# Forty unread products on TensorE in steps 5 to 9 of the first stage of a Hyena + FFN block

## What is computed

```
xn  = layernorm(x)                               # over the 256 channels
h   = layernorm(xn) * gamma + beta
v, x1, x2 = split(h @ W_in + b_in, 3)            # each 4096 x 256
y   = causal_conv(v, k0) * x1                    # 128 taps per channel, along the tokens
y   = causal_conv(y, k1) * x2
att = xn + y @ W_out + b_out
ffn = (silu(xn @ wg.T) * (xn @ wu.T)) @ wd.T     # hidden 768, int weights times 1/127
out = x + att + ffn
```

## Time and profile before

| what | value |
|---|---|
| median of 3 runs | 351.94 us (351.06 to 352.59) |
| profiled execution | 351.36 us |
| its span | 349.5 us |
| mean granted clock of its span | 0.974 |
| PE busy | 307.8 us (88%) |
| PEld busy | 239.7 us (69%) |
| DVE busy | 247.0 us (71%) |
| POOL busy | 215.7 us (62%) |
| ACT busy | 181.8 us (52%) |

### The profile page before, as it was taken

One profiled execution on the slowest core, in us unless ns is written; L12 is line 12 of the kernel. 1 busy time (PEld: TensorE's weight loads), 2 busy tenths in 40 slices (PEclk: granted clock), 3 DMA queues, 4 the chain that ended last, 5 costly groups with the idle time before them and its releaser, 6 DMA issues.

```text
span 349.5 us, 11796 instructions
## 1 busy us (share of the span) xinstructions
PE 307.8 (88%) x4941; PEld 239.7 (69%) x4941; DVE 247.0 (71%) x498; ACT 181.8 (52%) x379; POOL 215.7 (62%) x302
## 2 busy tenths in 40 slices
PE   0767777776897999999999999999999999998995
PEld 0355666655775777777777777777777876657994
DVE  3996983555357577568567678867766966897895
ACT  3634886954335354443444444434544344549992
POOL 3979999302887888866876776777886782210000
PEclk9965998999999999999999999999999999999999
DMA  7990260006687957879578687786786969400445
GB/s 236 349 357 21 70 235 4 0 9 232 241 311 255 388 194 308 314 250 387 206 304 345 249 366 247 288 356 229 333 304 262 381 240 344 169 0 2 164 140 180
DMA packets 21506, 81.01 MB, mean 232 GB/s; under 512 B 1479, under 2 KB 12619, under 8 KB 13259
## 3 DMA queue, kind: packets, MB, share of 16 engines
q1 hardware_dynamic: 19458, 77.47, 59.3%
q0 software_dynamic: 1840, 2.36, 3.1%
q10 hardware_dynamic: 152, 0.40, 0.4%
HBM read 75.50 MB, written 4.72 MB: 229 GB/s over the span
## 4 chain that ended last, share of the span: by engine, by line
PE 44%; DVE 17%; POOL 15%; ACT 12%; issue 7%; DMA 2%; SPq 0%; POOLq 0%; DVEq 0%; ACTq 0%
PE bank_c L282 11%; PE bank_p L282 8%; PE bank_u L282 8%; PE bank_g L282 8%; PE bank_d L282 8%; ACT vx L734 3%; DVE hhl L934 3%; ACT vx L726 3%; POOL ybuf L1136 3%; DVE sgh L929 2%; DMA res<-in_L_attn_x 2%; POOL ybuf L1240 2%; POOL res L1187 2%; ACT hhl L664 2%; POOL res L1188 2%
## 5 line engine op out<-in xcount | busy, mean ns | idle before, releaser
L282 PE MATMUL bank_d<-wd,hhl 128*128 128x256 f16 x384 | 84.3, 271 | 0.3 <-DVE hhl L934 0.2
L282 PEld LDWEIGHTS bank_p<-wq,xT 128*128 128x128 f16 x1536 | 71.4, 99 | 14.5 <-issue 0.3
L282 PE MATMUL bank_p<-wq,xT 128*128 128x64 f16 x1536 | 80.6, 194 | 0.2 <-issue 0.2
L282 PE MATMUL bank_u<-xT,wgu 128*128 128x512 f16 x192 | 66.2, 378 | 0.4 <-DVE sgh L929 0.4
L282 PE MATMUL bank_g<-xT,wgu 128*128 128x512 f16 x192 | 66.2, 377 | 0.0
L282 PEld LDWEIGHTS bank_c<-ybuf,bands 128*128 128x128 f16 x1024 | 51.4, 96 | 21.2 <-issue 4.5
L282 PE MATMUL bank_c<-ybuf,bands 128*128 128x64 f16 (+3 forms) x1024 | 60.2, 184 | 3.8 <-DVE ybuf L954 3.8
L282 PEld LDWEIGHTS bank_c<-vhl,bands 128*128 128x128 f16 x1024 | 49.0, 96 | 18.5 <-issue 3.1
L282 PE MATMUL bank_c<-vhl,bands 128*128 128x64 f16 (+3 forms) x1024 | 57.3, 184 | 2.1 <-DVE x1y L788 0.9
L664 ACT CAST hhl<-sgh 128x512 f16<-128x512 f32 x48 | 29.7, 619 | 47.2 <-DVE sgh L929 47.2
L1144 POOL TENSOR_TENSOR vx<-vx,bias 128x512 f32<-128x512 f32 x32 | 37.8, 1184 | 25.2 <-DVE vx L796 25.2
(11 more groups left out here) (177 smaller groups left out, 557.3 us busy)
## 6 DMA issues: line engine op xcount, KB each, us to landing
bands<-taps_seq SPq DMA_DIRECT2D x64, 1024.0 KB, 8.1
out<-res SPq DMA_DIRECT2D x8, 512.0 KB, 2.9
res<-in_L_attn_x SPq DMA_DIRECT2D x3, 1024.0 KB, 10.9
res<-in_L_attn_x SPq DMA_DIRECT2D x2, 512.0 KB, 6.2
bands<-in_L_attn_W_in SPq DMA_DIRECT2D x1, 768.0 KB, 6.2
bands<-in_L_ffn_w_gate POOLq DMA_DIRECT2D x1, 768.0 KB, 7.3
bands<-in_L_ffn_w_up POOLq DMA_DIRECT2D x1, 768.0 KB, 8.8
vx<-in_L_ffn_w_down POOLq DMA_DIRECT2D x1, 768.0 KB, 9.9
```

The lines of the kernel that those rows point to most:

```text
L282: return nc.tensor.matmul(o, w, m, start=start, stop=stop, skip_group_check=True)
```

## The change

A helper `keep_busy(n)` issues n products of 128 x 128 by 128 x 256 in float16 into the first 256 columns of `bank_c[1]`. Their operands are the high half of blocks 0 and 1, long in place. In steps 5, 6, 7, 8 and 9 PE issues eight of them, right behind the transposes of that step and ahead of everything else in it. Nobody reads what they write, no semaphore is counted up, and no wait is added or taken away. In all there are forty products and forty weight loads more.

```diff
+            def keep_busy(n):
+
+                for _ in range(n):
+                    mm(bank_c[1][:, 0:2 * P], xT[:, 0, 0:P], xT[:, 0, 0:2 * P], True, True)
+
             def first_stage(b):
                 if b < NB:
                     transpose_x(b)
+                if 5 <= b < LX + 2:
+                    keep_busy(8)
                 if b == 2:
                     beta_weights()
```

## The result

The changed kernel took 356.68 us (median of 4, 356.25 to 357.65) against 352.26 us of the kernel before beside it (median of 4, 351.06 to 352.93). The ratio is 1.013, with a 95% interval of 1.0086 to 1.0175. Run again later beside more executions of before, it took 355.34 us (9 executions) against 352.34 us (32), a ratio of 1.0091 (1.0056 to 1.0126). So it is slower by 3.0 to 4.4 us, and both intervals lie wholly on the slow side by over 0.5%. I had forecast 352.3 us with a range of 350.9 to 353.6.

A forecast was written before the change was run, and what follows sets the result against it. POOL's chain was taken to bound the first stage; PE 1.5 us late at step 10, less 1.15 of room, gave +0.35: profiled 351.36 became 351.7, and with the median 0.58 above the profiled run, 352.3 us; range 350.9 to 353.6.

The forecast's parts named there:

- The path that I priced: PE late at step 10 delays DVE, then max_mm, step 19, ACT's copy of block 19 and the fork: +0.35 us.
- What bounds the kernel.: From 23.9 to 54 us POOL's normalisations and scale computations set the pace; faster PE in steps 5 to 9 gains 0.
- The price of eight products.: In each of steps 5 to 9, eight products cost PE 1.68 us at low clock, 0.88 at high.
- The rise of the clock.: PE's clock in the first stage returns at about 31 us instead of 34.5, with bounds of 24 and 34.5.
- Who is made late.: POOL isn't late and ACT recovers; DVE carries 1.5 us, max_mm waits 0.7, step 19 is 0.55 late, fork 0.35.
- The branch takes its 3.36 us: At the fork ahead of step 22, the branch keeps its length of 3.36 us.
- nothing else is added: no wait, no transfer: In steps 5 to 9, forty products cost only 4.4 to 8.4 us of PE time, with no further wait or transfer.
- The slower rival: Clock rises no sooner than 34.5 us, step 10 is 3.1 us late, the fork 1.9: 353.8 us; chance 0.13.
- The faster one: Clock stays up behind the fork, steps 22 and 23 run faster, perhaps 1.0 us is passed on: 350.9; chance 0.08.
- The first: Step 5's products lift the clock at about 24 us; PE then waits for others, no gain: 351.9 us; chance 0.27.

The follow-up runs named there:

- the same place of code: Kernel before with 256 unexecuted instructions, 351.43 us, and changed kernel with 176 unexecuted instructions, 351.98 us; their taken copies lie at the same address.
- flipped kernel: Kernel before with the two copies behind the fork in the other order, the taken copy directly after the branch: 351.57 us, ratio 0.9988.
- the moved code alone: Kernel before with 80 unexecuted PE instructions at the head of the copy not taken, moving the taken copy down: 354.62 us, ratio 1.0081.

## Why the prediction was wrong

The path that I priced is there in the profiles, at +0.35 us forecast; the medians with the same place of code give 0.55, which is within noise, and the profiles 0.8 us at the second stage's start. It was the smaller part of the loss. Step by step:

**What bounds the kernel.** Right. POOL's chain did not move, and no time was won from the earlier rise.

**The price of eight products.** Right: 1.70 and 0.88 us against 1.68 and 0.88. So were the positions that followed from it, offset taken off: step 6 at 27.06 (27.04 forecast), step 7 at 29.57 (29.52), step 8 at 31.97 (31.6), step 9 at 33.93 (33.5), step 10 at 35.99 (35.5).

**The rise of the clock.** Forecast at 31, seen at 32.0. That is the 0.4 to 0.5 us by which steps 8 to 10 were later. The second profile of the same kernel had it at 29.8, so 31 was as good a guess as one profile allows. I would not read the difference to before's 34.5 as the products' work alone. The flipped kernel without any had the clock back at 32.6 in its profile (granted 0.72 from 32 to 33 us), and the changed kernel with 176 instructions added at 32.7. Seven profiles without the products have it between 32.6 and 35.2, five with eight a step between 29.8 and 32.7.

**Who is made late.** Right by name. `max_mm` waited 0.76 us (0.7 forecast), step 19 was 0.68 late (0.55), the read of the flag 0.6 (0.35). Not foreseen was a wait of 1.16 us in step 16, for DVE's `pm_ready`; it is the same lateness of DVE, met two steps earlier.

**"The branch takes its 3.36 us".** This is the step that failed. I took the length of the branch for a constant of the fork and never asked what it consists of. I had the row, a COMPARE_BRANCH of 3358 ns, and knew that its target lies thousands of instructions away in the second copy. A compare takes no such time; the flipped kernel's took 86 ns. The 3.27 us between the two are the wait for code: a packet of instructions is fetched within them, and none where the branch is not taken. What then is at hand depends on where the code lies. From there "nothing else is added: no wait, no transfer" was wrong too, since 80 instructions are themselves added to what has to be fetched, and shift all that comes behind. The list of what would make me wrong named "the branch itself costs another time because the code in front of it is longer", with no price and no chance. It should have been the slower rival: with the first block's remainder too short to cover the next transfer, PE stands for what is left of it, 1.65 us here, and the steps around it run at the low clock. What the runs showed in its place: 1.65 and 2.06 us of standing in step 22 in the two profiles of the changed kernel, and 2.6 us for the moved code alone. A bound of 0 to one more branch time, 3.4 us, on top of the sum reaches 355.7. It would have held the second measurement, 355.34, and missed the first by 1.0 us.

**The slower rival** that I did put up, a clock that rises no sooner, did not happen. That its 353.8 us was on the side of the result is no merit. **The faster one**, the second dip gone, did not happen either with the change as it stands. It did in the kernels whose taken copy follows the branch, and in two profiles with the far branch: before with 256 instructions added, whose second stage then started 1.13 us earlier (1.0 was my figure), and the one with sixteen products a step. In both PE had stood 2.8 to 2.9 us at the fork, so standing there does not by itself bring the clock down, as the prediction has it. **The first**, a rise at 24 us, was seen once, at 25.7 with sixteen products a step.

**The range** was built from one mechanism and its neighbours. It ended at 353.6, because every case in it was about when PE's array is busy.

What stays open is why the first four executions lost 4.4 us, 1.3 more than these two parts. Their profile has a third stretch at the low clock, near 74 us, which goes with 0.68 us. The changed kernel's second profile doesn't have it, and two with added code do (from 71.9 and from 70.2), so it comes and goes. The second measurement, 3.0 us, needs no third part.

## What to carry to other kernels

Code that is added ahead of a taken branch moves the branch's target in its block of instructions, and that can cost more than the code itself does (2.6 us of moved code here, against 0.55 us or nothing for forty products). So price a branch by what it must fetch, and test an edit's own worth with unexecuted code that puts the target back where it was. Put the copy that is always taken right behind the branch, and let the jump over the other copy come when nobody waits for the engine any more. Look at the end of the trace then: here the last transfer out landed 1.2 us late beside the jump.

Filling an engine to keep its clock up was worth nothing here, where another engine sets the pace. Find in the chain who would be waiting for the faster steps before asking what the clock would give.

## What the runs showed of the hardware that I had not expected

- A branch whose target is far away took 3.3 to 3.9 us on PE, and a branch not taken, into the code directly behind it, 0.08 to 0.09 us. Each far one was over 2.3 to 2.8 us after the start of a packet of 16 KB of instructions. A far jump at PE's end took 4.5 to 4.7 us, and in both kernels that have it the last transfer out landed 1.2 us late.
- Behind a far jump the next block comes late. With the target's block ending 16 instructions on (two products of 8 columns, two transposes, three products of `project`, their loads, a wait and one that the trace doesn't list), PE stood 1.65 to 2.06 us; with 16 more instructions in hand 0.37 us; with 96 in hand none. PE went on 2.2 to 2.4 us after the start of the packet.
- Waits for code showed in straight code as well, most of them in `project_beside`, where products of 64 columns follow each other at 0.03 us: PE stood 0.2 to 1.6 us at up to six places. The shift has a say in where: with 80 instructions more, three profiles agree in stalls of 1.4 to 1.55 us near 109 and 0.4 to 0.7 us near 222. But it doesn't decide alone, since two profiles of the changed kernel have three and five such stalls and share only these two. Before had one, of 0.17.
- Whether the clock falls behind the fork, where PE stands 2.7 to 3.3 us, is not fixed by the length of the standing: in two of ten profiles with a far branch (2.76 and 2.93 us) it stayed up. Nor is the moment of its rise in the first stage fixed by the code: 32.0 and 29.8 us in two profiles of one kernel.
- The kernel's executions scatter over 5 us (349.85 to 354.80 in 32 executions of before), and the slower ones tend to have the lower mean clock: the median clock is 0.974 in the faster sixteen and 0.966 in the slower sixteen. An effect of half a per cent needed a dozen executions here.
